# Head attention by key tiles: how the last tile's value products are split, and where the output is taken

## The chip, the cores and the metric

One NeuronCore of a Trainium2 chip runs the whole program. The metric is the device time of one execution in microseconds (us), start to end. The profile is one execution seen by the hardware profiler; its span runs from the first to the last instruction. Engines: PE is TensorE's matmuls and PEld its weight loads, DVE is VectorE, ACT is ScalarE, POOL is GpSimd, SP is SyncE, which here only issues transfers.

## The reference, cut to what matters

The program is one layer over x of 4 x 1024 tokens of width 256, all in fp32: a causal attention branch over the normalised x, and a branch with a 16-head attention (head width 16), a gated feed-forward part with a shared and eight routed experts, and norms. The change lies in the 16-head attention:

```python
attn = jnp.einsum('bhqd,bhkd->bhqk', q, k) / np.sqrt(DH)     # B=4, H=16, T=1024, DH=16
attn = jax.nn.softmax(attn, axis=-1)
sa = jnp.einsum('bhqk,bhkd->bhqd', attn, v)
sa = sa.transpose(0, 2, 1, 3).reshape(Bb, Tt, C) @ Wo
```

## The kernel before, in words

The stages follow one another: projections, causal attention, head attention (`head_attention`, some 300 to 1024 us of the profile), feed-forward. Only head attention is touched.

**Steps, halves, units.** A step is one batch entry and a group of GH = 4 heads; there are STEPS = 16. A step has NQ = 2 halves of the queries, CH = 512 each (index c), and each half runs over QT = 8 key tiles of 128 (index j). One half and one key tile are a unit; a step has UNITS = 16 of them, w = c * 8 + j, and the stage has 256, counted by u.

**Scores and exponentials.** For a unit, `score` (L1428) makes four 128 x 512 score tiles, keys on the partitions and queries in the columns, one per head, as two pairs (p = 0, 1) that sit side by side in the rows of the array. They go to three PSUM banks `h_sk` in turn (`bank_at`, BANKS = 3; in the last step the two banks of `sq[0]` are added). A pair waits on `exp_done` until both of its banks are emptied (L1436), so a unit's first pair needs the second and third exponential of the unit before, and its second pair the first exponential of its own unit. ACT's `fill` (L1502) turns each tile into exponentials in `probs[u % 2]` (`h_p`, L1507) and counts `exp_done`. The first fill of a unit waits until the unit two before has been multiplied (`pv_done`).

**Value products.** `mix` (L1443) multiplies the exponentials of a unit with the values of its key tile. Four products, one per head, of 32 output rows each (16 of values, 16 of ones, which give the sum of the exponentials), lie side by side in the columns of the array and fill the 128 partitions of the one PSUM bank `po` (`h_po`, 512 columns), in which the eight key tiles of a half are added up. An fp32 product shows as two records. `mix` is called twice per unit, with part 0 and 1 (PARTS = 2). For the key tiles 0 to 6 each part takes 256 of the 512 queries. For the last one (`last`, j = 7) part 0 returns at once and part 1 takes all 512.

**Taking the output.** When a half is done, ACT copies `po` to `outT[c]` (`take_out`, L1510 to L1514: waits for `pv_done`, counts `out_taken`) and issues the store of it (`store`, L1516 to L1518: waits for `out_taken`). The first product of the next half waits for `out_taken` (L1450) before it may overwrite `po`. Every first part also waits until all four exponentials of its unit are there (L1456).

**Row maxima for the next step.** Beside this, PE makes the scores of the step after once more, in the other orientation and without the shift by the maximum (`item`, L1409, tiles `h_sq`, two buffers), and DVE takes their row maxima (`maximum`, L1538, TENSOR_REDUCE at L1541), two items per unit. Once a step DVE joins the halves (L1548), PE turns the maxima (`turn_maxima`, L1422) and DVE splits them in two terms (L1557, L1562).

**The order on PE** is written out by hand: for each unit u, for part 0 and part 1, the score pair of u, an item that is LEAD = 4 units ahead, and a part of the products of the unit before, u - 1:

```python
for part, coming in enumerate(ahead):
    if n < STEPS:
        score(n, w, part)
    ...
    if coming[0] < STEPS:
        item(*coming)
    if u:
        mix(*divmod(u - 1, UNITS), part)
```

**The order on ACT** is one loop over all fills f, four per unit. With TAKE = GH = 4, the take-out stands behind fill 32k + 3, the fourth exponential of the first unit of the next half, and the store behind fill 32k + 4.

Of the kernel before, what the change touches and what calls it, by code (L numbers as in the profile page):

```python
# [16 lines left out]
CH = 512  # L17
# [4 lines left out]
GH = 4  # L22
# [8 lines left out]
QT = S // P  # L31
# [1201 lines left out]
def head_attention(nc, inputs, ot_d, ffw, chunk, routing):  # L1233
# [3 lines left out]
    with ExitStack() as ctx:  # L1237
# [8 lines left out]
        UNITS = NQ * QT  # L1246
# [3 lines left out]
        PARTS = PAIRS  # L1250
# [4 lines left out]
        PR = 2  # L1255
# [3 lines left out]
        probs = [sb(f"h_p{i}", [P, GH, CH]) for i in range(PR)]  # L1259
# [47 lines left out]
        def item_slot(n, m):  # L1307
            return n * ITEMS + m + max(0, n - 1 + (n >= 1 and m >= HELD))

        def turn_slot(n):  # L1310
            return (n + 1) * ITEMS + n + (HELD if n + 1 < STEPS else 0)
# [8 lines left out]
        with nc.Block() as block:  # L1320
# [86 lines left out]
            @block.tensor  # L1407
            def _(pe):
                def item(n, m):  # L1409

                    p, i, half = m // (QT * NQ), m // NQ % QT, m % NQ
                    r, slot = n % RING, item_slot(n, m)
                    if m == 0 and n >= AHEAD:
                        pe.wait_ge(loaded[r], loads_of(n) if n % RING >= AHEAD else loads_of(n) - LOADS * 16)
                    pe.wait_ge(sq_free[slot % 2], slot // 2)
                    for g in range(SIDES):
                        at = slice(g * SIDE_AT, g * SIDE_AT + DOTS)
                        ins = nc.tensor.matmul(sq[slot % 2][:, g, :], q6[r][at, p, i * P:(i + 1) * P],  # L1418
                                               k6[r][at, p, half * CH:(half + 1) * CH], start=True, stop=True)
                    ins.then_inc(sq_made, 1)  # L1420

                def turn_maxima(n):  # L1422
                    slot = turn_slot(n)
                    pe.wait_ge(max_done, n + 1)
                    pe.wait_ge(sq_free[slot % 2], slot // 2)
                    nc.tensor.transpose(sq[slot % 2][0:TILES, 0, 0:P], negm, ident).then_inc(sq_made, 1)

                def score(n, w, p):  # L1428

                    c, j = divmod(w, QT)  # L1430
                    r, f = n % RING, n * FILLS + w * GH + p * SIDES
                    if w == 0 and p == 0:
                        pe.wait_ge(shifted[r], shifts_of(n))
                    emptied = [before[f + g] for g in range(SIDES) if before[f + g] is not None]
                    if emptied:
                        pe.wait_ge(exp_done, max(emptied) + 1)  # L1436
                    for g in range(SIDES):
                        at = slice(g * SIDE_AT, g * SIDE_AT + ROWS)
                        ins = nc.tensor.matmul(spread_banks[bank_at(f + g)], k6[r][at, p, j * P:(j + 1) * P],  # L1439
                                               q6[r][at, p, c * CH:(c + 1) * CH], start=True, stop=True)  # L1440
                    ins.then_inc(scored, 1)

                def mix(n, w, part):  # L1443


                    c, j = divmod(w, QT)
                    u, last = n * UNITS + w, j == QT - 1
                    if part == 0:
                        if j == 0:
                            pe.wait_ge(out_taken, n * NQ + c)  # L1450
                        if w == 0 and n >= AHEAD:
                            pe.wait_ge(spread, n - AHEAD + 1)
                        if last:
                            return
                    if part == 0 or last:
                        pe.wait_ge(exp_done, (u + 1) * GH)  # L1456
                    at = slice(0, CH) if last else slice(part * CH // PARTS, (part + 1) * CH // PARTS)

                    for h in range(GH):
                        ins = nc.tensor.matmul(po[h * VW:(h + 1) * VW, at], vh[n % RING][:, j, h, :],  # L1460
                                               probs[u % PR][:, h, at], start=j == 0 and part == 0, stop=last)
                    if part == PARTS - 1:
                        ins.then_inc(pv_done, 1)

                def first_way(w):
                    if w == 1:
                        pe.wait_ge(routing.const_set, Routing.CONSTS)
                    if 1 <= w <= TPC:
                        routing.out_projection(pe, 0, first, [w - 1])
                    if w == TURN_AT:  # L1470
                        routing.turn_tokens(pe, 0, first)
                    if w == GATES_AT:
                        routing.gates(pe, 0, first)
                    if w == COUNT_AT:
                        routing.count(pe, 0, first)

                for m in range(ITEMS):
                    item(0, m)
                for m in range(HELD):
                    item(1, m)  # L1480
                pe.wait_ge(const_set, 2)
                turn_maxima(0)
                for m in range(HELD, LEAD * PER):
                    item(1, m)
                for u in range(STEPS * UNITS + 1):
                    n, w = divmod(u, UNITS)
                    ahead = [divmod(u * PER + ITEMS + LEAD * PER + b, ITEMS) for b in range(PER)]
# [3 lines that stand above are left out]
                        if part == 0 and coming[1] == HELD and coming[0] <= STEPS:  # L1491
                            turn_maxima(coming[0] - 1)
# [4 lines that stand above are left out]
                    if n == STEPS - 1:  # L1497
                        first_way(w)

            @block.scalar  # L1500
            def _(act):
                def fill(f):  # L1502
                    u, h = divmod(f, GH)
                    if h == 0 and u >= PR:
                        act.wait_ge(pv_done, u - PR + 1)
                    act.wait_ge(scored, f // SIDES + 1)
                    nc.scalar.activation(probs[u % PR][:, h, :], spread_banks[bank_at(f)], ACT.Exp,  # L1507
                                         scale=DH ** -0.5).then_inc(exp_done, 1)

                def take_out(n, c):  # L1510
                    act.wait_ge(pv_done, n * UNITS + (c + 1) * QT)
                    if n:
                        act.wait_ge(stored[c], n * 16)
                    nc.scalar.activation(outT[c][:, :], po[:, :], ACT.Copy).then_inc(out_taken, 1)  # L1514

                def store(n, c):  # L1516
                    act.wait_ge(out_taken, n * NQ + c + 1)
                    act.dma_start(ot_d[n, :, c * CH:(c + 1) * CH], outT[c][:, :]).then_inc(stored[c], 16)  # L1518

                TAKE = GH  # L1520
                HALF = QT * GH
                for f in range(STEPS * FILLS + TAKE + 1):
                    if f < STEPS * FILLS:
                        fill(f)
                    if f == LAST + ROOT_AT * GH:
                        routing.root(act, 0)
                    if f == LAST + EXP_AT * GH:
                        routing.exponentials(act, 0)
                    if f >= HALF and (f - TAKE + 1) % HALF == 0:
                        take_out(*divmod((f - TAKE + 1) // HALF - 1, NQ))  # L1530
                    if f > HALF and (f - TAKE) % HALF == 0:
                        store(*divmod((f - TAKE) // HALF - 1, NQ))
                for c in range(NQ):
                    act.wait_ge(stored[c], STEPS * 16)
# [516 lines left out]
```

## Time and profile before

| what | value |
|---|---|
| median of three runs | 1583.39 us (1582.5 to 1584.44) |
| profiled execution, its own time | 1580.62 us |
| its span, mean granted clock | 1578.8 us, 0.964 |
| busy over the span | PE 92%, PEld 54%, DVE 76%, ACT 53%, POOL 23% |
| L1541, DVE row maxima | 512 of 1224 ns, 621.9 us |
| L1507, ACT exponentials | 999 (and 25 from the added banks) of 595 ns |
| L1460, PE value products | 3840 records, 324.3 us |
| L1514, ACT take-outs | 32 |

The profile counts an engine as busy while any instruction of it runs; records of one engine can overlap, as neighbouring matmuls do, and as two activations in a row do on ACT. The timeline merges like instructions of an engine that follow without a gap into one line. "[idle before <- releaser]" is how long the engine stood idle before the line and what released it.

### The profile page before, as it was taken

What the parts mean: (1) busy time and instruction counts of PE and PEld (TensorE: products, weight loads), DVE (VectorE), ACT (ScalarE), POOL (GpSimd) and SP (SyncE); (2) the same over time, 40 slices, a digit from 0 to 9 for tenths busy, and PEclk for the clock granted to TensorE, in tenths of its full rate; (3) what the DMA queues carried; (4) which work ended last, traced back from release to release, by engine and by line L of the source; (5) the groups of instructions that cost most, each with busy time, mean ns of one, the idle gap of its engine ahead of it and who ended that gap; (6) DMA issues with size and microseconds to landing.
All of it is one profiled execution on the core that took longest, in us unless ns stands there. A gap on an engine that the chain in (4) does not pass through costs nothing. (4 is left out here: it accounts for less than half of the span.)

```text
span 1578.8 us, 25397 instructions
## 1 busy us (share of the span) xinstructions
PE 1454.6 (92%) x9648; PEld 852.5 (54%) x9648; DVE 1203.6 (76%) x1733; ACT 839.3 (53%) x1507; POOL 368.2 (23%) x314
## 2 busy tenths in 40 slices
PE   7998799779999999999999999769999999999994
PEld 4565577523333333333333333358787887878873
DVE  3776766699999999999999996447677676776532
ACT  2454344118888888888888888621413314123130
POOL 0435902243320000000000000022325244252441
PEclk9999899859999999999999999889999999999997
DMA  6799766331543343433333311032031230321211
GB/s 200 272 319 347 258 185 141 70 82 48 102 89 62 61 62 62 62 62 62 56 62 62 63 55 37 26 101 80 18 106 33 76 97 18 102 42 41 55 14 14
DMA packets 105845, 146.12 MB, mean 93 GB/s; under 512 B 24048, under 2 KB 74624, under 8 KB 105728
## 3 DMA queue, kind: packets, MB, share of 16 engines
q1 hardware_dynamic: 84480, 107.13, 26.7%
q0 software_dynamic: 10784, 23.76, 6.9%
q10 hardware_dynamic: 10464, 13.64, 2.8%
q8 instruction: 78, 1.28, 0.4%
q14 instruction: 39, 0.32, 0.1%
HBM read 80.90 MB, written 63.06 MB: 91 GB/s over the span
## 5 line engine op out<-in xcount | busy, mean ns | idle before, releaser
L1541 DVE TENSOR_REDUCE i_saT<-h_sq 128x2 f32<-128x1024 f32 x512 | 621.9, 1224 | 34.4 <-PE h_sq L1418 22.1
L1507 ACT ACTIVATE h_p<-h_sk 128x512 f32<-128x512 f32 x999 | 543.3, 595 | 143.9 <-PE h_sk L1439 121.6
L1460 PE MATMUL h_po<-h_p,h_v 128*32 128x256 f32 (+1 forms) x3840 | 324.3, 410 | 7.4 <-ACT h_o L1514 4.8
L1439 PE MATMUL h_sk<-h_q,h_k 50*128 50x512 f32 x999 | 255.1, 501 | 16.6 <-ACT h_p L1507 16.0
L1418 PE MATMUL h_sq<-h_k,h_q 48*128 48x512 f32 x1024 | 222.3, 429 | 20.9 <-DVE i_saT L1541 17.0
L1439 PEld LDWEIGHTS h_sk<-h_q,h_k 50*128 50x128 f32 x999 | 95.5, 185 | 241.6 <-ACT h_p L1507 232.4
L1764 PE MATMUL f_ob<-w_experts,f_h 128*128 x768 | 179.1, 392 | 0.0
L1460 PEld LDWEIGHTS h_po<-h_p,h_v 128*32 128x32 f32 x3840 | 75.8, 108 | 181.7 <-issue 85.1
L1764 PEld LDWEIGHTS f_ob<-w_experts,f_h 128*128 128x128 f32 x768 | 143.7, 188 | 31.3
L1677 POOL TENSOR_TENSOR f_h<-h_place,f_h 128x512 fp32r<-128x512 f32 x64 | 83.9, 1317 | 288.5 <-ACT f_h L1829 288.5
L1825 ACT ACTIVATE f_x1p<-f_pair 128x1024 fp32r<-128x1024 f32 x8 | 8.2, 1026 | 225.5 <-PE f_pair L1068 225.5
L1418 PEld LDWEIGHTS h_sq<-h_k,h_q 48*128 48x128 f32 x1024 | 102.3, 196 | 43.1 <-DVE i_saT L1541 38.7
L1339 POOL COPY h_v<-h_values 128x512 f32<-128x512 f32 x14 | 8.6, 612 | 474.0 <-DMA h_values<-vh_d 447.0
L1836 ACT ACTIVATE h_place<-f_pair 128x512 f32<-128x512 f32 x64 | 38.3, 598 | 126.6 <-PE f_pair L1756 124.9
L1756 PE MATMUL f_pair<-f_x1p,w_routed 128*128 128x512 f32 x384 | 93.5, 402 | 5.8 <-DVE h_place L1123 5.4
L1756 PE MATMUL f_pair<-f_x1p,w_shared 128*128 128x512 f32 x384 | 95.3, 400 | 2.1 <-DVE h_place L1888 2.1
L1888 DVE TENSOR_TENSOR h_place<-h_place,f_pair 128x512 f32<-128x512 f32 x64 | 43.3, 685 | 66.8 <-ACT h_place L1836 61.6
L1756 PEld LDWEIGHTS f_pair<-f_x1p,w_routed 128*128 128x128 f32 x384 | 72.9, 190 | 23.6 <-issue 6.2
L1896 DVE SCALAR_TENSOR_TENSOR h_place<-f_ob,h_v,h_place 128x256 f32<-128x256 f32 x128 | 61.8, 483 | 30.7 <-PE f_ob L1764 25.7
L1756 PEld LDWEIGHTS f_pair<-f_x1p,w_shared 128*128 128x128 f32 x384 | 70.4, 188 | 20.2 <-DVE h_place L1888 4.9
L746 PE MATMUL a_out<-a_v,a_pT 128*128 128x256 f32 x432 | 65.5, 305 | 7.1 <-DVE a_v L827 7.1
L719 PE MATMUL a_sc<-c_kT,c_qT 128*128 128x512 f32 (+3 forms) x192 | 68.1, 492 | 2.3 <-PEq L288 2.3
(211 smaller groups left out, 1734.3 us busy)
## 6 DMA issues: line engine op xcount, KB each, us to landing
h_q<-q_d SPq DMA_DIRECT2D x84, 128.0 KB, 5.8
h_k<-k_d SPq DMA_DIRECT2D x84, 128.0 KB, 6.7
ot_d<-h_o ACTq DMA_DIRECT2D x32, 256.0 KB, 3.3
q_d<-t_parts SPq DMA_DIRECT2D x12, 512.0 KB, 4.9
k_d<-t_parts SPq DMA_DIRECT2D x12, 512.0 KB, 5.1
h_place<-xs_d SPq DMA_DIRECT2D x8, 530.0 KB, 4.2
p_xin<-in_L_attn_x SPq DMA_DIRECT2D x8, 512.0 KB, 5.0
xn_d<-p_xn SPq DMA_DIRECT2D x8, 512.0 KB, 4.8
```

Source lines behind the costliest of these rows:

```text
L719: ins = nc.tensor.matmul(sc[u % 2][:, c:c + w], qT[b % 2][:, k, i * P:(i + 1) * P], kT[b % 2][:, k, c:c + w], start=k == 0, stop=k == KD - 1)
L746: ins = nc.tensor.matmul(out[u % 2][:, 0:D], pT[u % 2][left][:, j, :], vp[b % 2][right][:, j, :], start=j == 0 and n == 0, stop=j == i and ...
L1418: ins = nc.tensor.matmul(sq[slot % 2][:, g, :], q6[r][at, p, i * P:(i + 1) * P], k6[r][at, p, half * CH:(half + 1) * CH], start=True, stop ...
L1439: ins = nc.tensor.matmul(spread_banks[bank_at(f + g)], k6[r][at, p, j * P:(j + 1) * P], q6[r][at, p, c * CH:(c + 1) * CH], start=True, sto ...
L1460: ins = nc.tensor.matmul(po[h * VW:(h + 1) * VW, at], vh[n % RING][:, j, h, :], probs[u % PR][:, h, at], start=j == 0 and part == 0, stop= ...
L1507: nc.scalar.activation(probs[u % PR][:, h, :], spread_banks[bank_at(f)], ACT.Exp, scale=DH ** -0.5).then_inc(exp_done, 1)
L1541: nc.vector.tensor_reduce(halfmax[n % 2][:, m, :], sq[slot % 2][:, :, :], AX.X, ALU.max)\
L1677: nc.gpsimd.tensor_tensor(h[LO][:, f, :], whole[f % 2], h[HI][:, f, :].bitcast(F32), ALU.subtract).then_inc(h_split, 1)
L1756: ins = nc.tensor.matmul(ps[:, half, :], w[a][:, k, at:at + P], x1p[b][:, k, :], start=n == 0, stop=n == len(terms) - 1)
L1764: ins = nc.tensor.matmul(to, lhs(left, i), weight(right, i), start=n == 0, stop=n == len(terms) - 1)
L1888: nc.vector.tensor_tensor(whole[f % 2], sil[f % 2], fills.buffer(key)[:, 1, :], ALU.mult)\
L1896: ins = nc.vector.scalar_tensor_tensor(xs[c % 2][:, j, 0:D], ob[b][:, i * D:(i + 1) * D], wm[:, j, 2 * g + i:2 * g + i + 1], xs[c % 2][:, ...
```

## The change

`mix` loses its special case: all eight key tiles are multiplied by halves of the queries, a part each. The last tile's part 0 is no longer skipped, and waits for the unit's exponentials; its part 1 takes the second 256 queries. `pv_done` is still counted by the last product of part 1, and `stop` is set on the last tile's second part alone. `TAKE` becomes GH - 1 = 3: the take-out stands behind fill 32k + 2, the third exponential of the first unit of the next half, and the store behind fill 32k + 3, the fourth. Nothing else differs.

```diff
                 def mix(n, w, part):
 
-
                     c, j = divmod(w, QT)
-                    u, last = n * UNITS + w, j == QT - 1
+                    u, last = n * UNITS + w, PARTS - 1
                     if part == 0:
                         if j == 0:
                             pe.wait_ge(out_taken, n * NQ + c)
                         if w == 0 and n >= AHEAD:
                             pe.wait_ge(spread, n - AHEAD + 1)
-                        if last:
-                            return
-                    if part == 0 or last:
                         pe.wait_ge(exp_done, (u + 1) * GH)
-                    at = slice(0, CH) if last else slice(part * CH // PARTS, (part + 1) * CH // PARTS)
+                    at = slice(part * CH // PARTS, (part + 1) * CH // PARTS)
 
                     for h in range(GH):
                         ins = nc.tensor.matmul(po[h * VW:(h + 1) * VW, at], vh[n % RING][:, j, h, :],
-                                               probs[u % PR][:, h, at], start=j == 0 and part == 0, stop=last)
-                    if part == PARTS - 1:
+                                               probs[u % PR][:, h, at], start=j == 0 and part == 0,
+                                               stop=j == QT - 1 and part == last)
+                    if part == last:
                         ins.then_inc(pv_done, 1)
...
-                TAKE = GH
+                TAKE = GH - 1
                 HALF = QT * GH
                 for f in range(STEPS * FILLS + TAKE + 1):
```

## Rows read from the trace of the kernel before

**Rows 1.** Groups by line and shape, 370 to 960 us: busy us, mean ns | idle before.
```profile
L1541 DVE TENSOR_REDUCE i_saT<-h_sq 128x2 f32<-128x1024 f32 x455 | 555.7, 1224 | 25.5 <-PE h_sq L1418 13.4
...
L1460 PE MATMUL h_po<-h_p,h_v 128*32 128x256 f32 x3168 | 253.0, 391 | 1.5
...
L1460 PE MATMUL h_po<-h_p,h_v 128*32 128x512 f32 x232 | 30.9, 605 | 0.0
L1514 ACT ACTIVATE h_o<-h_po 128x512 f32<-128x512 f32 x29 | 17.3, 597 | 5.0 <-PE h_po L1460 5.0
```

**Rows 2.** Windows: us, busy PE, PEld, DVE, ACT, POOL, PE clock, DMA share, GB/s.
```profile
358.70:974.00 615.30, 594.53 (x5459) 213.54 (x5455) 584.82 (x518) 529.23 (x977) 41.68 (x50) 1.00 0.35 63
1000.40:1007.20 6.80, 6.80 (x42) 2.27 (x39) 0.00 (x0) 4.08 (x8) 0.00 (x0) 0.50 0.11 41
```

**Rows 3.** Waits, 370 to 960 us: who <- for whom: us, times, longest.
```profile
PEld h_sk L1439 <- ACT h_p L1507: 212.1, 440, 1.0
...
DVE i_saT L1541 <- PE h_sq L1418: 13.4, 31, 0.4
...
PEld h_sq L1418 <- DVE i_saT L1541: 5.6, 14, 0.4
```

**Rows 4.** Timeline of PE, 702.6 to 712.3 us: start, length, what.
```profile
702.63 0.50 PE L1439 MATMUL h_sk<-h_q,h_k 50*128 50x512 f32 x2
702.96 0.40 PE L1418 MATMUL h_sq<-h_k,h_q 48*128 48x512 f32 x2
703.88 0.51 PE L1439 MATMUL h_sk<-h_q,h_k 50*128 50x512 f32 x2 [0.51 <-ACT h_p L1507]
704.22 0.40 PE L1418 MATMUL h_sq<-h_k,h_q 48*128 48x512 f32 x2
704.55 1.06 PE L1460 MATMUL h_po<-h_p,h_v 128*32 128x512 f32 x8
705.55 0.50 PE L1439 MATMUL h_sk<-h_q,h_k 50*128 50x512 f32 x2
...
706.33 0.64 PE L1460 MATMUL h_po<-h_p,h_v 128*32 128x256 f32 x8
706.90 0.50 PE L1439 MATMUL h_sk<-h_q,h_k 50*128 50x512 f32 x2
...
708.13 0.50 PE L1439 MATMUL h_sk<-h_q,h_k 50*128 50x512 f32 x2
...
709.38 0.50 PE L1439 MATMUL h_sk<-h_q,h_k 50*128 50x512 f32 x2
...
710.61 0.50 PE L1439 MATMUL h_sk<-h_q,h_k 50*128 50x512 f32 x2
```

**Rows 5.** Timeline of DVE at two boundaries between halves.
```profile
373.60 1.23 DVE L1541 TENSOR_REDUCE i_saT<-h_sq 128x2 f32<-128x1024 f32 x1 [0.45 <-PE h_sq L1418]
...
706.32 7.53 DVE L1541 TENSOR_REDUCE i_saT<-h_sq 128x2 f32<-128x1024 f32 x6 [0.43 <-PE h_sq L1418]
```

**Rows 6.** Timeline of ACT around the same boundary (ACTq: its DMA issues).
```profile
700.75 2.27 ACT L1507 ACTIVATE h_p<-h_sk 128x512 f32<-128x512 f32 x4 [0.20 <-PE h_sk L1439]
...
703.23 0.60 ACT L1507 ACTIVATE h_p<-h_sk 128x512 f32<-128x512 f32 x1 [0.20 <-PE h_sk L1439]
...
704.42 1.09 ACT L1507 ACTIVATE h_p<-h_sk 128x512 f32<-128x512 f32 x2
705.68 0.60 ACT L1514 ACTIVATE h_o<-h_po 128x512 f32<-128x512 f32 x1 [0.17 <-PE h_po L1460]
706.18 0.59 ACT L1507 ACTIVATE h_p<-h_sk 128x512 f32<-128x512 f32 x1
706.31 0.33 ACTq L1518 DMA_DIRECT2D ot_d<-h_o  x1
706.68 0.60 ACT L1507 ACTIVATE h_p<-h_sk 128x512 f32<-128x512 f32 x1
```

**Rows 7.** Timeline of PE in the last step, at its middle boundary.
```profile
1000.28 1.02 PE L1460 MATMUL h_po<-h_p,h_v 128*32 128x256 f32 x8 [3.97 <-ACT h_o L1514]
```

## The prediction

> **What bounds the kernel now.** I read the costliest groups first, over the stretch in which all 29 like boundaries lie: DVE's row maximum leads, 455 times 1224 ns [rows 1], and that alone suggests DVE as the bound. The windows correct it: from 358.70 to 974.00 us, at full clock, PE is busy for 594.53 of 615.30 us, DVE for 584.82, ACT for 529.23 [rows 2]. The waits then say who waits for whom: DVE waits 31 times for PE's items, 13.4 us in all; PE waits 440 times for ACT's exponentials, but for DVE only some 6 us [rows 3]. So DVE follows PE, and PE's queue, with its waits for ACT, sets the pace.
>
> A unit (one key tile, 512 queries, four heads) takes 2.48 us. On PE it has two parts, each of a score pair, a row-maximum item and value products: scores start at 708.13, 709.38 and 710.61, so 1.25 and 1.23 apart [rows 4]. The item starts 0.33 or 0.34 after the scores, the products 0.33 after the item, the next scores 0.57 after narrow products (706.33 to 706.90). A unit's second scores need the bank that its first exponential empties; in the longer gap PE waits some 0.02 us for it.
>
> Time is lost at the boundary between two halves of the queries. DVE idles 0.45 us before 373.60 and 0.43 before 706.32 [rows 5]; there are 29 such boundaries, as the 29 take-outs and the 232 (29 times 8) wide product records count them [rows 1], and 29 x 0.43 = 12.5 us makes up nearly all of DVE's 13.4. That is the prize that one could hope for.
>
> I call the half's last unit A and the next ones B, C, D; "1" and "2" are a unit's first and second score pair, e1 to e4 its exponentials. One boundary now [rows 4, 6]: B1 at 702.63, its item at 702.96, no products in this part; B2 at 703.88, behind e1 of B, which ends at 703.83, plus 0.05 (PE idle 0.51); its item at 704.22; A's last products over all 512 columns from 704.55 to 705.61; C1 at 705.55; the take-out from 705.68 to 706.28; e1 of C at 706.18, the store's issue at 706.31 for 0.33, e2 of C at 706.68; B's first products at 706.33, 0.05 behind the take-out; C2 at 706.90; D1 at 708.13. From B1 to D1 that is 5.50 us, where two undisturbed units take 4.96. So a boundary costs 0.54: 0.43 because the wide products hold PE for 1.00 us to the next scores where narrow ones hold it for 0.57, and 0.11 for the wait for the take-out.
>
> **Part 1, the last tile's products by halves.** Removed: four products of 512 columns (eight records of 605 ns). Added: twice four of 256 (391 ns) [rows 1]. The first four go behind B1's item: 702.96 + 0.33 = 703.29. Their input is A's e4, which ended at 703.02 (700.75 plus 2.27 [rows 6]); it is there. They let the next scores go 0.57 later, at 703.86, while B2 waits for e1 until 703.88 anyway: cost 0, hidden by PE's idle 0.51; without that cover it would be 0.57. The second four start at 704.55 as now and end at 705.19 (0.64 [rows 4]); C1 goes at 705.12 instead of 705.55, and e3 of B, which it needs, ends at 705.02 (704.42 + 0.60 [rows 6]). **Gain so far 0.43.**
>
> The new switch between the scores' array layout and the products' is what the trace doesn't show at this place. Bounds: 0, as at all switches now (the scores start at 706.90, 0.07 before the products end at 706.97 [rows 4]), and 0.07 if the next scores have to wait for that end. I take 0, since wide products show the same overlap (705.55 against 705.61). The Trainium skill's TensorEngine Tiling (Array Packing), Tiling Modes, says that a change of tiling mode drains TensorE, which speaks against one more switch per boundary; by it the sum would be that of rival 3. The overlap in this trace shows no full drain.
>
> **Part 2, the take-out one exponential earlier.** It waits for the products' end plus 0.07 (705.61 to 705.68): 705.26 instead of 705.68, and ends at 705.86. But ACT works its queue in order, so **e4 of B** now stands behind the waiting take-out. Now it starts at 704.91 (the pair from 704.42 takes 1.09, one of them 0.60 [rows 6]). After the change it follows the take-out by 0.50 (705.68 to 706.18), so at 705.76, and lasts 0.59, to 706.35: 0.85 later. Its reader is PE: B's first products wait for all four exponentials of B, not only for the take-out. They start at 706.35 + 0.05 = **706.40**; PE would be free for them at 705.12 + 0.33 + 0.33 = 705.78, and now they start at 706.33. Behind them in PE's queue are C2, its item and B's second products. C2 then is at 706.40 + 0.57 = 706.97 (now 706.90), and D1, 1.23 later, at **708.20 (now 708.13)**. So the 0.43 is given back at the very next wait, and 0.07 more: what is late next is e4 of B.
>
> Other waits that could end last. The store's issue moves with the take-out, to stand between e4 of B and e1 of C. ACT's second exponential behind a take-out starts 1.00 after it with the issue between them (705.68 to 706.68): e1 of C at 706.26, done 706.86, seen by C2 at 706.91, before 706.97. e3 of C follows C2 by 0.54 (703.88 to 704.42) and ends at 708.11, seen at 708.16, before D1. DVE: the item of C1 comes 0.43 earlier, that of C2 0.07 later, so its idle time moves by one item; its own work is 1.22 per item where PE's pace is 1.24, so it neither gains nor binds. SP and POOL wait for the last products of a step, which end 0.42 earlier at every second boundary; both load for a later step, and PE waits for neither in these rows.
>
> **Sum.** 29 x 0.07 = +2.0 us. In the last step there are no items and five banks: B's products wait at 1000.28 for the take-out [rows 7]. With the exchanged order an exponential stands in the same place of ACT's queue, so 0 to 0.1 for each of its two boundaries; and the very last products cost 2 x 0.57 - 1.00 = 0.14 more, partly beside DVE's work for the next stage. I take 0.1 together: **+2.1 us**. The profiled execution took 1580.62 us (span 1578.8), so 1582.7 for one like it. The median of the three runs lies 2.8 above it, and in that measure the forecast is 1583.39 + 2.1 = **1585.5**. What a measurement can tell from no change here is 0.2%, 3.2 us, or 0.11 per boundary.
>
> **Rivals.**
> 1. *Faster: e4 isn't what ends last* (chance 0.11). If e4 of B were done in time, B's products would wait for the take-out alone: 705.86 + 0.05 = 705.91, C2 at 706.48, D1 at 707.71, 0.42 per boundary, -12.2 us, 1571. For it: the gap of 0.43 plainly comes from PE's wide products. Against: ACT's rows stand in the order of the code, and the take-out of now holds e1 of C in just this way.
> 2. *The half clock near the end falls elsewhere* (0.09). From 1000.40 to 1007.20 PE has clock 0.50 [rows 2], 1.2 GHz, after it idled 3.97 us [rows 7]. PE is busy for all of those 6.80 us; at the full clock much of it would take half, so up to 3 us are to be had: in sum -0.9, 1582.5. Against: the idle itself, from the table load and the root on ACT, stays. The Trainium skill's TensorE: Matmul & The Clock Gate, Part 1, says that the watch on activity runs free of the program; so the phase may differ between any two executions.
> 3. *Slower by the layout switch* (0.15). If scores wait for the end of the added products, B2 is at 703.29 + 0.64 + 0.01 = 703.94 instead of 703.88; its item, the second products, the take-out, e4 and C2 all follow 0.06 later: 0.13 per boundary, +3.8, 1587.2. It decides from a delay of 0.02 on, all the slack between 703.86 and 703.88.
> 4. *Slower by the store's issue* (0.10). If it were issued only when e4 of B has ended, e1 of C would start at 706.35 + 0.03 + 0.33 + 0.05 = 706.76 and end at 707.36, C2 at 707.41: 0.51 per boundary, +14.8, 1598. It decides once e1 of C ends after 706.92. Against: now it goes at 706.31, 0.03 behind the take-out, in the middle of e1 of C.
>
> **How the numbers follow.** Forecast 0.55. Its five read terms (0.07, 0.50, 0.59, 0.05, 0.57) have a hundredth or so each: 0.02 to 0.12 per boundary, +0.6 to +3.5. With rivals 2 and 3 in, the change is -0.9 to +3.8; executions of before reach from 1580.62 to 1584.44, so a median is good to about 1.4: 1581.1 to 1588.6. Rivals 1 and 4, together 0.21, stay outside. Faster: rival 1 and a little of rival 2, 0.13. Slower: rival 4, two thirds of rival 3 and 0.09 from the forecast's upper end, 0.29. Same: 0.58.
>
> **What would show it.** Right: the wide products are gone; the take-out starts 0.07 behind the products' end, with one exponential fewer ahead of it; B's first products are released by an exponential, not by the take-out; DVE's idle of some 0.5 stands one item later, its total near 13 us as now. Wrong: B1 to D1 under 5.4 us (rival 1) or over 5.62 (3 or 4); B2 more than 1.27 behind B1 (3); the store's row behind e4's end (4).

## The result, and the profile after

The changed kernel takes 1592.74 us (median of 18 runs, 1587.92 to 1602.55), the kernel before in the same comparison 1585.45 us (18 runs, 1580.0 to 1597.22): ratio 1.0045, interval 1.0026 to 1.0064, so slower by 0.45%. The forecast was 1585.5, 0.13% above the 1583.39 it started from. The profiled execution has a span of 1591.3 us. Four of the executions in the experiments below took over 1.5% longer than the fastest of their kernel; they are left out of every median, ratio and fit.

The groups of the changed kernel by line and shape, 372 to 966 us, its 29 boundaries with items (busy us, mean ns | idle before):

```profile
L1538 DVE TENSOR_REDUCE i_saT<-h_sq 128x2 f32<-128x1024 f32 x454 | 554.6, 1224 | 29.5 <-PE h_sq L1418 21.2
...
L1456 PE MATMUL h_po<-h_p,h_v 128*32 128x256 f32 x3632 | 290.3, 391 | 18.3 <-ACT h_p L1504 18.3
...
L1511 ACT ACTIVATE h_o<-h_po 128x512 f32<-128x512 f32 x29 | 17.3, 598 | 6.7 <-PE h_po L1456 6.7
```

Against [rows 1] the wide products are gone, the narrow ones cost 391 ns as before, and there is a new wait: 18.3 us in which the value products wait for ACT's exponentials. The waits view of the same stretch gives its count:

```profile
PEld h_po L1456 <- ACT h_o L1511: 30.1, 29, 1.0
DVE i_saT L1538 <- PE h_sq L1418: 21.2, 31, 0.7
PE h_po L1456 <- ACT h_p L1504: 18.3, 29, 0.6
```

29 waits of 0.63 us for an exponential, one per boundary. DVE's wait for items rose from 13.4 [rows 3] to 21.2 us.

PE's timeline around one boundary, the same one as [rows 4]:

```profile
707.07 0.50 PE L1439 MATMUL h_sk<-h_q,h_k 50*128 50x512 f32 x2
...
707.73 0.64 PE L1456 MATMUL h_po<-h_p,h_v 128*32 128x256 f32 x8
708.32 0.50 PE L1439 MATMUL h_sk<-h_q,h_k 50*128 50x512 f32 x2
...
708.98 0.64 PE L1456 MATMUL h_po<-h_p,h_v 128*32 128x256 f32 x8
709.54 0.50 PE L1439 MATMUL h_sk<-h_q,h_k 50*128 50x512 f32 x2
709.88 0.40 PE L1418 MATMUL h_sq<-h_k,h_q 48*128 48x512 f32 x2
710.91 0.64 PE L1456 MATMUL h_po<-h_p,h_v 128*32 128x256 f32 x8 [0.63 <-ACT h_p L1504]
711.48 0.50 PE L1439 MATMUL h_sk<-h_q,h_k 50*128 50x512 f32 x2
...
712.72 0.50 PE L1439 MATMUL h_sk<-h_q,h_k 50*128 50x512 f32 x2
```

In the prediction's names (A is the last unit of a half, B, C and D the next ones, 1 and 2 a unit's score pairs): B1 707.07, A's first half of products 707.73, B2 708.32 (1.25 behind B1, as now), A's second half 708.98, C1 709.54 (1.22 behind B2 instead of 1.67: the 0.43 is gained), then B's products only at 710.91, C2 at 711.48, D1 at 712.72. From B1 to D1 that is 5.65 us against 5.50. ACT's timeline, for the same boundary:

```profile
707.67 1.79 ACT L1504 ACTIVATE h_p<-h_sk 128x512 f32<-128x512 f32 x3 [0.20 <-PE h_sk L1439]
709.68 0.60 ACT L1511 ACTIVATE h_o<-h_po 128x512 f32<-128x512 f32 x1 [0.23 <-PE h_po L1456]
710.18 0.59 ACT L1504 ACTIVATE h_p<-h_sk 128x512 f32<-128x512 f32 x1
710.31 0.33 ACTq L1515 DMA_DIRECT2D ot_d<-h_o  x1
```

Three exponentials of B, the take-out waiting 0.23 us for A's products, and the fourth exponential behind it, ending at 710.77. The products start **0.14 us after that end**, where [rows 4, 6] have 0.05 from a take-out's end to the products. And DVE's timeline:

```profile
712.25 1.23 DVE L1538 TENSOR_REDUCE i_saT<-h_sq 128x2 f32<-128x1024 f32 x1 [0.71 <-PE h_sq L1418]
```

One gap of 0.71 stands where before there was one of 0.43 and, one item later, one of 0.13 (the end of the maximum at 706.32 to the start of the next at 707.67), too short to be listed as a wait. DVE's whole idle time before its maxima rose from 25.5 [rows 1] to 29.5 us: by 4.0, or 29 times 0.14.

**Not all of it lies there.** From the first to the 29th take-out it is 586.35 us (374.69 to 961.04) against 582.39 (372.95 to 955.34), both at the full clock throughout: +4.0 us over 28 halves, 0.14 each. From the 31st to the 32nd it is 30.4 us against 22.7. The windows of the changed kernel there, and of the kernel before (us, busy PE, PEld, DVE, ACT, POOL, PE clock, DMA share, GB/s):

```profile
981.00:1005.60 24.60, 20.90 (x178) 8.30 (x178) 5.99 (x10) 20.06 (x37) 0.00 (x0) 1.00 0.15 54
1005.60:1036.00 30.40, 29.07 (x182) 11.26 (x182) 8.02 (x37) 16.41 (x33) 0.97 (x1) 0.56 0.03 9
```

```profile
975.10:999.60 24.50, 20.13 (x168) 8.04 (x168) 5.69 (x9) 19.99 (x37) 0.00 (x0) 1.00 0.16 54
999.60:1022.30 22.70, 21.29 (x174) 8.81 (x174) 6.42 (x30) 15.53 (x32) 0.00 (x0) 0.85 0.03 12
```

The work is nearly the same (182 and 174 records), but the mean clock is 0.56 instead of 0.85. In the changed kernel's execution the clock stood at half from 1005.9 to 1016.2 and from 1019.6 to 1050.3; before, from 1000.4 to 1007.2 and from 1024.3 to 1037.9. Whether the change does that, or the execution, these two profiles can't say; those of the experiments can.

### The profile page after: what moved, and what is told of

Same layout as the page of the kernel before. It is cut to its first block and busy times, and to the rows that moved or that the text cites. A ratio compares the mean times of both kernels' runs of the same rounds, so it can differ in the third digit from the quotient of the medians.

```text
span 1591.3 us, 25909 instructions
## 1 busy us (share of the span) xinstructions
PE 1467.5 (92%) x9904; PEld 861.4 (54%) x9904; DVE 1204.2 (76%) x1733; ACT 841.8 (53%) x1507; POOL 368.6 (23%) x314
## 5 line engine op out<-in xcount | busy, mean ns | idle before, releaser
L1538 DVE TENSOR_REDUCE i_saT<-h_sq 128x2 f32<-128x1024 f32 x512 | 622.0, 1223 | 38.3 <-PE h_sq L1418 29.9
L1456 PE MATMUL h_po<-h_p,h_v 128*32 128x256 f32 x4096 | 335.5, 400 | 23.3 <-ACT h_p L1504 23.3
L1456 PEld LDWEIGHTS h_po<-h_p,h_v 128*32 128x32 f32 x4096 | 82.5, 109 | 209.0 <-issue 98.5
```

The costliest lines, as they stand in the source:

```text
L1538: nc.vector.tensor_reduce(halfmax[n % 2][:, m, :], sq[slot % 2][:, :, :], AX.X, ALU.max)\
```

## The experiments

To compare kernels in spite of the clock there are two measures. The first is the stretch from the first to the 29th take-out in the profile: 28 halves, at the full clock from end to end in every kernel but the last of the table. It is one execution each, but holds no half clock. The second uses all executions. I took from each execution its time at the half clock, 2 x (1 - mean granted clock) x span, and fitted the 138 executions whose clock is known (the 18 first ones of the kernel before have none) with one slope for all and a level for each kernel. The slope is 0.36 us of time per us at the half clock (0.38 with the four long executions in, the figure of an expectation below), the scatter around it 1.8 us. Read at 130 us of half clock, the kernel before stands at 1588.1 and 1588.8 (32 executions on one chip, beside the first four kernels that follow the change in the table, and 23 on another, beside the last two), mean 1588.4. The last column below is against that; its uncertainty is about 0.6 us.

| kernel | B1 to D1, us (median of 29) | 1st to 29th take-out, us | median us | ratio to before (interval) | at equal half clock |
|---|---|---|---|---|---|
| before | 5.50 | 582.39 | 1585.45; 1590.54; 1593.72 | | 1588.4 |
| the change | 5.65 | 586.35 | 1592.74 | 1.0045 (1.0026 to 1.0064) | +3.9 |
| halves alone | 5.22 | 574.47 | 1580.14 | 0.9932 (0.9902 to 0.9962) | -9.4 |
| early take-out alone | 6.08 | 598.02 | 1605.77 | 1.0084 (1.0050 to 1.0117) | +15.6 |
| the change, waits swapped | 5.57 | 583.84 | 1592.14 | 1.0012 (0.9978 to 1.0046) | +0.7 |
| before, waits swapped | 5.59 | 584.45 | 1595.61 | 1.0025 (0.9987 to 1.0062) | +1.8 |
| the change again | 5.66 | 586.06 | 1595.21 | 1.0025 (0.9996 to 1.0055) | +3.7 |
| the change in the last step alone | 5.51 | 587.49 (half clock up to 397.2) | 1589.28 | 0.9976 (0.9950 to 1.0003) | +0.5 |

The three medians of the kernel before belong to three sets of runs: 1585.45 for the change, 1590.54 for the next four kernels, 1593.72 for the last two. By their intervals alone, four of the seven kernels can't be told from before.

**Halves alone.** The changed kernel with

```diff
-                TAKE = GH - 1
+                TAKE = GH
```

> All value products by halves as in the change, but the output taken behind the fourth exponential of the next unit, as before. Theory 1 (the fourth exponential, pushed behind the take-out, is what costs): the take-out starts 0.49 us behind the start of the fourth exponential, at 0.16 after where it starts in the changed kernel; the next unit's first products are released by it, and two units around a boundary take 5.23 us instead of 5.50 (before) and 5.64 (after). 29 boundaries x -0.27 = -7.8 us against before, about 1577 to 1579. Rival (the halves themselves cost, by array switches or by clock): no gain against before, boundary 5.45 us or more.

Measured: 5.22 us per boundary (expected 5.23), 1580.14 us, 0.7% faster than before. Between the first and the 29th take-out it takes 7.9 us less, against 7.8 expected for the boundaries; the 9.4 at equal half clock are 1.5 more, which nothing here explains. Its PE timeline at a boundary, from B2's products on, and ACT's:

```profile
681.19 0.64 PE L1456 MATMUL h_po<-h_p,h_v 128*32 128x256 f32 x8
681.76 0.49 PE L1439 MATMUL h_sk<-h_q,h_k 50*128 50x512 f32 x2
682.09 0.39 PE L1418 MATMUL h_sq<-h_k,h_q 48*128 48x512 f32 x2
682.70 0.64 PE L1456 MATMUL h_po<-h_p,h_v 128*32 128x256 f32 x8 [0.21 <-ACT h_o L1511]
```

```profile
680.37 1.79 ACT L1504 ACTIVATE h_p<-h_sk 128x512 f32<-128x512 f32 x3
682.04 0.60 ACT L1511 ACTIVATE h_o<-h_po 128x512 f32<-128x512 f32 x1
682.52 0.62 ACT L1504 ACTIVATE h_p<-h_sk 128x512 f32<-128x512 f32 x1
```

The take-out starts 0.21 after the products' end instead of 0.07, because the fourth exponential is ahead of it; but B's products then need only the take-out, wait 0.21 instead of 0.63, and start 0.61 behind the item instead of 1.03. The halves are a gain of 0.28 per boundary, and the early take-out takes it away and 0.15 more.

**Early take-out alone.** The kernel before with `TAKE = GH - 1` and nothing else.

> The last key tile's products stay over all 512 queries; only the take-out goes behind the third exponential. Theory 1: the fourth exponential now waits for products that end 0.43 us later than with halves, the next products start another 0.43 us later: two units around a boundary take 6.07 us instead of 5.50, 29 x 0.57 = +16.5 us against before, about 1602. Rival (the early take-out costs little by itself, the halves do): 5.5 to 5.6 us per boundary and within 3 us of before.

Measured: 6.08 us per boundary (expected 6.07), +15.6 us between the take-outs and +15.6 at equal half clock. Its PE waits for the exponential (ending at 704.00) after ACT waited 0.65 us for the wide products:

```profile
701.78 1.07 PE L1460 MATMUL h_po<-h_p,h_v 128*32 128x512 f32 x8
702.78 0.50 PE L1439 MATMUL h_sk<-h_q,h_k 50*128 50x512 f32 x2
703.11 0.40 PE L1418 MATMUL h_sq<-h_k,h_q 48*128 48x512 f32 x2
704.15 0.64 PE L1460 MATMUL h_po<-h_p,h_v 128*32 128x256 f32 x8 [0.63 <-ACT h_p L1507]
```

```profile
702.92 0.60 ACT L1514 ACTIVATE h_o<-h_po 128x512 f32<-128x512 f32 x1 [0.65 <-PE h_po L1460]
703.41 0.59 ACT L1507 ACTIVATE h_p<-h_sk 128x512 f32<-128x512 f32 x1
```

So the moved take-out costs 0.58 a boundary on wide products and 0.43 on halves (5.65 against 5.22). The 15.6 us are 1.0%, inside the interval of the ratio, 0.5 to 1.2%.

**The waits swapped.** Both kernels wait, ahead of a half's first products, for the take-out and for the exponentials. The changed kernel with the opposite order (and the kernel before with the same swap):

```diff
                     if part == 0:
-                        if j == 0:
-                            pe.wait_ge(out_taken, n * NQ + c)
+                        pe.wait_ge(exp_done, (u + 1) * GH)
                         if w == 0 and n >= AHEAD:
                             pe.wait_ge(spread, n - AHEAD + 1)
-                        pe.wait_ge(exp_done, (u + 1) * GH)
+                        if j == 0:
+                            pe.wait_ge(out_taken, n * NQ + c)
```

> The changed kernel with the three waits ahead of a unit's first products in the opposite order in the program: exponentials first, take-out last. Theory 1 (of several waits only one is carried by the weight load itself; the others are instructions of their own on PE, and the one that ends last costs 0.14 us from the exponential's end to the products instead of 0.05): release to start falls from 0.14 to 0.05 us and the boundary from 5.64 to 5.55, 29 x -0.09 = -2.6 us against the changed kernel. Rival (a product block that starts on a fresh exponential takes 0.14 whichever way it waits): unchanged, 5.64.

> The kernel before with the same swap of the waits. Theory 1: now the wait for the take-out, which ends last there, may move to an instruction of its own or stay, according to which one the weight load carries: if it moves, 0.14 instead of 0.05 from the take-out's end to the products and 29 x 0.09 = +2.6 us. Rival: nothing changes, 5.50 us per boundary, same time as before.

Measured, over all 29 boundaries, from the end of what is waited for to the first product: the change 0.143 to 0.144 us, with the swap 0.052 to 0.053; the kernel before 0.052 to 0.053, with the swap 0.144 to 0.146. In the changed kernel's timeline above the fourth exponential ends at 710.77 and the products start at 710.91. These are ACT's and PE's timelines of the swapped one, where that exponential ends at 696.86:

```profile
696.27 0.59 ACT L1504 ACTIVATE h_p<-h_sk 128x512 f32<-128x512 f32 x1
...
696.91 0.64 PE L1456 MATMUL h_po<-h_p,h_v 128*32 128x256 f32 x8 [0.55 <-ACT h_p L1504]
```

And those of the kernel before with the swap, where the take-out ends at 693.85 and the products start 0.144 us later (693.998):

```profile
693.25 0.60 ACT L1514 ACTIVATE h_o<-h_po 128x512 f32<-128x512 f32 x1 [0.17 <-PE h_po L1460]
...
694.00 0.64 PE L1460 MATMUL h_po<-h_p,h_v 128*32 128x256 f32 x8
```

The swap takes 0.09 off in one kernel and adds it in the other. Per boundary that is 5.57 instead of 5.65 (5.55 expected) and 5.59 instead of 5.50; between the take-outs 2.5 us less than the change (2.6 expected) and 2.1 more than before (2.6 for theory 1); at equal half clock 3.2 less and 1.8 more. Both rivals fall: the delay follows the order of the waits, not what is waited for. Even so mended, the change is no faster than the kernel before: 1.4 us more between the take-outs. In the changed kernel a separate instruction stands in the queue of PE's weight loads (PEldq) for line 1452, the wait for the exponentials:

```profile
L1452 PEldq EVENT_SEMAPHORE  x1: 51/51/51, 710.8 to 710.8; - x1
```

It takes 51 ns from 710.80, just after the exponential's end. In the swapped one line 1452 is the wait for the take-out, and its separate instruction is through long before the exponential ends:

```profile
L1452 PEldq EVENT_SEMAPHORE  x1: 51/51/51, 696.4 to 696.4; - x1
```

In each kernel there are 32 of them, one per half, all at the line of the later wait and none at that of the first. So of the two waits the later one in the program is an instruction of its own, and it costs 0.09 us when that one ends last. That the weight load carries the first is inferred: it is the next instruction in that queue. A half at the start of a step waits for a third signal, `spread`, as well; no separate instruction stands at its line, so how three waits are shared out stays open. It changes neither of the two times. In the kernel before the take-out ended last and was the first of the waits; the change made the exponentials end last without moving the waits.

**The change again.** The same kernel, beside new runs of the kernel before, on another chip than the four kernels above.

> The changed kernel once more, beside new runs of the kernel before on the same chip. Theory 1 (the 29 boundaries at +0.14 to 0.15 us are all that the change itself adds; the rest of the first difference of 7 us is how long the clock stood at half in either set): +4.2 us at equal time at the half clock, where over all runs so far a us more at the half clock goes with some 0.38 us more time. Rival (the change itself brings more half clock, by its longer waits): the changed kernel shows more time at the half clock than the kernel before again, by 10 us or so, and is 7 us slower.

Measured: 1.0025 (0.9996 to 1.0055), 1.5 us above before by the medians, +3.7 at equal half clock, and 586.06 us between the take-outs, 3.7 more than before. The median time at half clock is 137 us against 143 for the kernel before beside it; in the first runs of the change it was 134. So nothing bears out the rival, that the change brings more of the half clock. Its profiled execution had a span of 1584.5 us, 6.8 under the first one's, with 5.66 per boundary. It also settles the end of the stage: here the 31st and 32nd take-outs are 23.3 us apart, where the same kernel had 30.4 above, and the kernel before with its waits swapped has 29.9. That difference belongs to the execution, not to the change.

**The change in the last step alone.** The last tile's products stay wide for every half but the last of step 14 and the two of the last step, and TAKE is three only from the last step's fills on:

```diff
-                    u, last = n * UNITS + w, j == QT - 1
+                    u = n * UNITS + w
+                    last = j == QT - 1 and u < (STEPS - 1) * UNITS - 1
...
-                for f in range(STEPS * FILLS + TAKE + 1):
+                for f in range(STEPS * FILLS + TAKE):
+                    TAKE = GH if f < LAST else GH - 1
```

> The change made in the last of the 16 steps alone (its two boundaries and the end); steps 0 to 14 as before. Theory 1: nothing to be told from before: 0 to +0.3 us at equal time at the half clock, and 29 boundaries of 5.50 us. Rival (the last step, where PE idles behind the table load and the clock falls, is where the change costs): half or more of the 7 us, with more time at the half clock between 980 and 1060 us in most runs.

Measured: +0.5 us at equal half clock, no difference that these runs can tell, and 127 us at the half clock, less than any other kernel's median. In its profile the half clock of the stage's start lasted on to 397 us, where before it ended at 358.7. The window, with the columns as above:

```profile
350.00:397.00 47.00, 46.67 (x256) 14.72 (x252) 26.93 (x23) 24.48 (x45) 18.57 (x13) 0.50 0.18 51
```

One execution of this kernel has 38 us more of half clock at a place that the edit doesn't touch. The last step is not where the change costs.

## Why the prediction was wrong

**Right in mechanism.** That PE's queue and not DVE bounds this stage, that the halves give 0.43 us between B2 and C1, that the moved take-out pushes the fourth exponential behind itself and that B's products give the gain back at once: all of it is in the timeline, and the two runs that make one half of the change each show it (5.22 and 6.08 us, both within 0.01 of what was expected of them, by a working that already had the 0.14 below). B2 stayed 1.25 us behind B1, so the added products are hidden by PE's idle time.

**The term that was mis-sized** is the step "they start at 706.35 + 0.05 = 706.40". 0.05 was read at a take-out's end, and carried over to an exponential's end. It measured 0.143, because the wait that ends last is now a separate instruction; with the waits swapped it is 0.052. With 0.14 in its place the boundary is +0.15 to 0.16 us by the hundredths of the working, against a measured 0.14 to 0.15, and 29 of them are some +4.1 us instead of +2.0. I gave the five read terms a hundredth or so each; the upper end, +3.5, was too near. The threshold that I had named, 0.11 per boundary, was passed by this one term. So was the sign of being wrong, B1 to D1 over 5.62: it is 5.65, but through neither of the two rivals to which I had tied it.

**The level and the clock** make the rest of the miss in absolute time, and the larger part: with the term put right the forecast would have been 1583.39 + 4.2 = 1587.6, still inside the range of 1581.1 to 1588.6, and the measured 1592.74 outside. The forecast rested on the median of three runs, 1583.39; over 18 runs the kernel before has 1585.45, and in later comparisons 1590.54 and 1593.72, on the same code. I took 1.4 us for the uncertainty of a median and should have taken several. In sum: 1585.5, plus 2.1 for the level, plus 2.0 for the term, plus 3.1 that the first comparison shows beyond what the boundaries give, is 1592.7. Those last 3.1 us did not come back in the repeat, where the medians are 1.5 us apart in all. That they are half clock is an inference: the clock in the 18 runs of the kernel before isn't known.

**The rivals.** 1 (the fourth exponential does not decide) is refuted by 29 waits for it. 2 (the half clock falls elsewhere) was the right thing to look at with too small a size, and with no tie to the change: the time at the half clock differs from execution to execution by tens of us, for the same kernel, and swamps the effect of the change. 3 (the layout switch) is refuted: B2 is 1.25 behind B1 in the median of 29, as before, and starts at 708.32, ahead of the added products' end at 708.37, which is modelled; so no drain shows here either. 4 (the store's issue) is refuted: it goes at 710.31, in the middle of the fourth exponential. **The signs:** DVE's total was expected near 13 us and is 21.2; the time per boundary rose by 0.14, but a second idle time of 0.13 that wasn't listed as a wait before has merged into the first, 0.43 + 0.13 + 0.14 = 0.70.

## What to carry to other kernels

Before moving an instruction forward in an in-order queue, ask what then stands behind its wait, and who reads that: here the take-out came 0.43 us earlier and the exponential behind it 0.83 later (from B1, 3.11 us instead of 2.28), and the reader needed both. When two semaphores are waited for ahead of a matmul, put the one that ends last first in the program; look again at that order whenever a change makes another one last. Of the two halves of this change one alone (halves, take-out left where it was) beats the kernel before by 0.7%, and the change by more: try the parts of a change separately.

## What the runs showed of the hardware that I had not expected

- Ahead of a matmul that waits for both a take-out and exponentials, the later wait in the program is an instruction of its own in the queue of the weight loads. When it ends last, 0.143 to 0.146 us pass from its release to the first product; when the other one does, 0.052 to 0.053. It holds for both signals, in both kernels, at all 29 boundaries.
- PE's clock can differ much between executions of one program: the time at half clock ran from 110 to 173 us over 32 executions of the kernel before on one chip, and each us of it went with 0.36 us of time, so that a spread of 23 us (1578.46 to 1601.8) is nearly all clock. Fitted against it, the scatter falls to 1.8 us, and effects of 2 us show that the medians hide; they agree with the stretch between the take-outs, which runs at the full clock.
